# Perceiver encoder on one core: the feed-forward part and the last norm of the linear-attention encoder are worked inside its attention loop, and attention keeps to six accumulator banks

## The chip, the cores and the metric

The kernel runs on one core of a Trainium2 chip. The metric is the device time of one execution in microseconds (us). Engines are named as the profile names them: PE is TensorE (PEld its weight loads), DVE is VectorE, ACT is ScalarE, POOL is GpSimd, SP is SyncE, which issues the transfers. PSUM is the accumulator memory that PE writes, eight banks of 128 partitions x 512 floats.

## The reference

Input is x, 128 sequences of 32 rows with 128 features, and a context. Six blocks follow one another, each added to x. The change concerns the second alone, a Performer encoder layer:

```python
q, k, v = x @ Wq, x @ Wk, x @ Wv                  # 16 heads of 64
qf = exp(dash(q) - diag(q) - rowmax(dash(q))) + EPS_KERN
kf = exp(dash(k) - diag(k) - max over all of dash(k)) + EPS_KERN
attn = (qf (kf^T v)) / (qf sum(kf)),  attn_out = attn @ Wo
out1 = layernorm(x + attn_out, ln1_g, ln1_b)
h = elu(out1 @ W1 + b1)                           # 128 -> 512
return layernorm(out1 + (h @ W2 + b2), ln2_g, ln2_b)
```

Its x is the layer norm of the running x, and what it returns is added to the running x.

## The kernel before, in words

The 4096 rows are T = 32 tiles of 128 rows (four sequences each). `stage_performer` works the encoder in three blocks, one behind the other, with a barrier between them. In each block every engine has an order of its own, written out by hand, and the engines meet at semaphores.

The first block (`att`) makes the features of all keys once to find their largest value, and then runs `run(eng, step)`: step t works on tile t, and begins or ends its neighbours. The steps from -2 to 0 and from T-3 to T are written out; those between are a loop of two steps a turn, so that j = t % 2 picks between double buffers. In the numbering of the tile t, the PE order of a step is: output projection of tile t-1 (L1189), transposes of the query features (L1158 with `enc_eq`), transposes of the key features (L1158 with `enc_ek`), projection K of tile t+1 (`project`, L109 to L111: each product of two halved float32 operands is three passes), the scores (`scores`, L1168), projection V of t+1, projection Q of t+2, `values` (L1179), projection DQ of t+2 (the query features before the exponent). `project` names its pair of banks: BA = banks 0 and 1 for K and Q, BB = 2 and 3 for the query transposes and scores, BD = 4 and 5 for the key transposes and the output projection, BC = 6 and 7 for V and DQ. `values` writes banks 2 to 5.

DVE in a step: largest value of the query features of t+1 out of DQ's banks (`largest_q`, L1338), their sum with the diagonal (L1341), `residual` of t-1 (L1369), `exponent_q` of t+1 (L1345, reads DQ's banks and signals `sub_ok`), then `softened` of t (sum L1356, reciprocal L1358, division L1360, transpose L1363; it waits for the scores), `count` of t-1 (statistics, L1374), `diagonal` of the keys of t+1 (L1334), `exponent_k` (L1351), `diagonal` of the queries of t+2. ACT moves the projections out of PSUM, squares them and takes the exponents. POOL copies one tile a step (L1435).

The second block (`net`) takes groups of four tiles (NG = 8): it makes the folded weights and biases, the 32 tiles' mean and reciprocal deviation in one go (`rstd_dve`, L75 to L85, and a square root on ACT), normalises (`normal`, L1546), transposes (L1486), multiplies by W1 in two float32 passes of 512 columns for each quarter (`up`, L1492), builds the elu (ACT L1609 and L1616, DVE L1552), multiplies by W2 (`down`, L1499), adds (`result`, L1559) and counts (L1567). The third (`end`) does the last norm (L1672, L1681) and the sum into x (L1691, L1695). Behind it stands the barrier at L67 and then `stage_moe0`, whose POOL begins with a memset (L2133).

Of the kernel before, what the change touches and what calls it, by code (L numbers as in the profile page):

```python
# [1018 lines left out]
def stage_performer(nc, k, bufs, kept):  # L1019

    dn = float(DH0) ** -0.25
    with ExitStack() as ctx:
# [7 lines left out]
        with ExitStack() as att:  # L1030
# [19 lines left out]
            BA, BB, BD, BC = 0, 2, 4, 6  # L1050
# [48 lines left out]
            def run(eng, step):  # L1099

                def within(t):
                    return lambda d: 0 <= t + d < T

                for t in range(-2, 1):
                    step(t, t % 2, within(t), 1)
                with eng.Fori(0, (T - 4) // 2) as i:
                    step(2 * i + 1, 1, lambda d: True, i + 2)
                    step(2 * i + 2, 0, lambda d: True, i + 2)
                for t in range(T - 3, T + 1):
                    step(t, t % 2, within(t), T // 2)  # L1110

            @block.tensor
            def _(pe):
# [70 lines left out]
                def step(t, j, has, turns):  # L1184
# [7 lines left out]
                    if has(0):  # L1192
                        pe.wait_ge(eq_ok, t + 1)
                        turn(BB, eq[:, j, :], tq_mm)
                        pe.wait_ge(ek_ok, t + 1)
# [45 lines left out]
                pe.wait_ge(ev_ok, T)  # L1241
                run(pe, step)

            @block.scalar
            def _(act):
                half = dn * 0.5 ** 0.5

                def step(t, j, has, turns):
                    if has(0):
# [3 lines left out]
                        nc.scalar.activation(kfT[:, :], both(BD), ACT.Copy, bias=EPS_KERN).then_inc(kf_ok, 1)  # L1253
                    if has(1):
# [3 lines left out]
                        nc.scalar.activation(eq[:, 1 - j, :], eq[:, 1 - j, :], ACT.Exp).then_inc(eq_ok, 1)  # L1258
                    if has(0):
                        nc.scalar.activation(xr[:, j, :], at(k.x, t), ACT.Identity, bias=shift[:, bass.ds(t, 1)],  # L1260
                                             scale=k.rstd[:, bass.ds(t, 1)]).then_inc(xr_ok, 1)
                    if has(1):
                        act.wait_ge(v_mm, t + 2)
                        nc.scalar.copy(va[:, 1 - j, :], both(BC)).then_inc(va_ok, 1)
# [5 lines left out]
                    if has(0):  # L1270
                        act.wait_ge(o_mm, t + 1)
                        nc.scalar.copy(atT[:, :, :, :].rearrange("p c b n -> p b c n"),
                                       ps[:, BB:BB + SEQ, 0:256].rearrange("p b (c n) -> p b c n", n=N)).then_inc(at_ok, 1)
                    if has(1):
# [3 lines left out]
                        nc.scalar.activation(ek[:, :], ek[:, :], ACT.Exp, bias=negmx[:, 0:1]).then_inc(ek_ok, 1)  # L1278

# [51 lines left out]
            def _(dve):  # L1331
# [4 lines left out]
                def largest_q(t):  # L1336
                    dve.wait_ge(dq_mm, t + 1)
                    nc.vector.tensor_reduce(mx[:, :], heads(both(BC)), AX.X, ALU.max).then_inc(mx_ok, 1)  # L1338
# [4 lines left out]
                def exponent_q(t, j):  # L1343
                    dve.wait_ge(cc_ok, t + 1)
                    nc.vector.tensor_tensor(heads(eq[:, j, :]), heads(both(BC)),  # L1345
# [25 lines left out]
                def count(t):  # L1371
                    dve.wait_ge(res_ok, t + 1)
                    nc.vector.nop(nofuse=True)
                    nc.vector.bn_stats(at(k.stats, t), at(res, t))  # L1374

                def step(t, j, has, turns):
# [4 lines left out]
                    if has(1):  # L1381
                        exponent_q(t + 1, 1 - j)
                    if has(0):
                        softened(t)
                    if has(-1):
                        count(t - 1)
                    if has(1):
                        diagonal(dk, ksq, ksq_ok, dk_ok, t + 1)
                        exponent_k(t + 1, 1 - j, turns)
                    if has(2):  # L1390
                        diagonal(dq, qsq, qsq_ok, dq_ok, t + 2)

# [23 lines left out]
                for u in range(T):  # L1416
                    dve.wait_ge(ev_ok, u + 1)
                    nc.vector.tensor_reduce(tops[:, u:u + 1], held[u % NH][:, :], AX.X, ALU.max).then_inc(max_ok, 1)
                    if u % 4 == 2 and u // 4 < NG - 3:
                        normal(u // 4 + 3)  # L1420
                dve.wait_ge(max_ok, T)
# [8 lines left out]
            def _(pool):  # L1430
                def step(t, j, has, turns):
                    if has(2):
                        if has(0):
                            pool.wait_ge(v_mm, t + 1)
                        nc.gpsimd.tensor_copy(xt[:, j, :, :], xs[:, bass.ds(t + 2, 1), :, :].rearrange(  # L1435
                            "p t m q -> p (t m) q")).then_inc(xt_ok, 1)

# [12 lines left out]

                for g in range(NG):
# [4 lines left out]


        with ExitStack() as net:
            sb = lambda n, s: net.enter_context(nc.sbuf_tensor(f"net_{n}", s, F32))
            sem = lambda n: k.sem(f"net_{n}")  # L1460
            PART = 4
            NG = T // PART
            w1g, cols = sb("w1g", [P, FF]), bufs["cols"]
            up_bias, down_bias, b1p = sb("up_bias", [P, NF]), sb("down_bias", [P, NF]), sb("b1p", [P, NF])
            ones = sb("ones", [P, P])
            row = sb("row", [P, D])
            n4, nT = sb("n4", [P, 2, PART, D]), sb("nT", [P, 2, PART * P])
            low, m = sb("low", [P, 2, 512]), sb("m", [P, 2, 512])
            hT = sb("hT", [P, 2, NF, 512])
            (ln, w_mm, set_ok, n_ok, tr_mm, tr_ok, up_mm, low_ok, m_ok, h_ok, y_mm, y_ok, base_ok, sum_ok) = [sem(n) for n in (  # L1470
                "ln w_mm set_ok n_ok tr_mm tr_ok up_mm low_ok m_ok h_ok y_mm y_ok base_ok sum_ok").split()]
            T_B, U_B, Y_B = 0, 2, 6
            part_of = lambda a, g: a[:, bass.ds(PART * g, PART), :]
            block = net.enter_context(nc.Block())

# [1377 lines left out]
```

## Time and profile before

| what | value |
|---|---|
| median of three runs | 2589.21 us (2582.16 to 2591.71) |
| the profiled execution | 2586.26 us, its span 2584.2 us |
| PE busy | 2420.6 us, 94% of the span |
| DVE busy | 1671.5 us, 65% |
| ACT busy | 1451.9 us, 56% |
| POOL busy | 1048.9 us, 41% |
| the scores of tile 0 are first read by DVE at | 780.4 us |
| the scores of tile 31 are first read by DVE at | 1161.7 us |
| the third block of the encoder ends at | 1265.2 us |

The busy times are unions over the whole program, six blocks of which five are untouched. So the shares say little here, and the section of rows below keeps to the stretch from 760 to 1270 us. The columns in an answer of the timeline are start, length, engine, line, operation, what it writes and reads, how many instructions were merged, and in brackets the idle time before the first of them and who ended it.

### The profile page before, as it was taken

Reading aid. Unit: us, or ns where it says so; the run is one execution under the profiler, and the core shown is the slowest. Engines: PE = TensorE matmul, PEld = TensorE weight load, DVE = VectorE, ACT = ScalarE, POOL = GpSimd, SP = SyncE. Lnnn points to the kernel's source line nnn. Section 1 sums busy time; section 2 is a strip of 40 time slices with the busy share of each in tenths; the row PEclk is TensorE's granted clock in tenths of the full one; section 3 lists DMA queues with packets and bytes.
Section 4 is the critical chain, followed back from the end, with each engine's and each line's share of the span. In section 5 each row is a group of like instructions: output and inputs, shape, how many; then the busy total and the mean of one; then the engine's idle time right before and its main releaser. Section 6 shows DMA issues by size and latency. Waiting matters only on the chain. (4 is left out here: it accounts for less than half of the span.)

```text
span 2584.2 us, 95575 instructions
## 1 busy us (share of the span) xinstructions
PE 2420.6 (94%) x39473; PEld 2081.0 (81%) x39473; DVE 1671.5 (65%) x3176; ACT 1451.9 (56%) x4128; POOL 1048.9 (41%) x1152
## 2 busy tenths in 40 slices
PE   6999999999889999999589998999999989899999
PEld 5999999899768888886479996777777778888888
DVE  4777777677586767766555555777777757555553
ACT  4666666566466676665544445777777734422222
POOL 2444444344330000004344444666666623355555
PEclk9999999999999999998689998999999989799999
DMA  6544444444071111100200001101010010066564
GB/s 210 227 166 169 146 153 164 144 151 167 32 285 34 49 41 41 49 26 1 73 1 1 0 0 37 43 24 31 24 27 28 13 54 0 9 134 127 104 133 77
DMA packets 60323, 206.34 MB, mean 80 GB/s; under 512 B 6670, under 2 KB 20498, under 8 KB 51226
## 3 DMA queue, kind: packets, MB, share of 16 engines
q1 hardware_dynamic: 60188, 204.41, 25.9%
q8 instruction: 100, 1.64, 0.3%
q14 instruction: 35, 0.29, 0.0%
HBM read 182.88 MB, written 21.51 MB: 79 GB/s over the span
## 5 line engine op out<-in xcount | busy, mean ns | idle before, releaser
L579 POOL TENSOR_TENSOR l_pn<-l_probs,l_rden 128x1024 f32<-128x1024 f32 x128 | 242.3, 1893 | 409.0 <-DVE l_rden L415 409.0
L512 ACT ACTIVATE l_probs<-ps,l_nmax 128x257 f32<-128x257 f32 x512 | 236.3, 475 | 246.5 <-DVE l_nmax L409 231.5
L980 POOL TENSOR_TENSOR l_probs<-l_probs,l_rden 128x1024 f32<-128x1024 f32 x128 | 242.3, 1893 | 172.4 <-DVE l_rden L831 172.4
L916 ACT ACTIVATE l_probs<-ps,l_nmax 128x257 f32<-128x257 f32 x512 | 236.3, 474 | 59.7 <-DVE l_nmax L825 59.7
L409 DVE TENSOR_REDUCE l_nmax<-ps 128x2 f32<-128x514 f32 x256 | 165.2, 686 | 124.8 <-PE ps L291 124.8
L2735 POOL TENSOR_TENSOR m_hh<-m_hh,m_cb 128x512 f32<-128x512 f32 (+1 forms) x136 | 179.6, 1322 | 142.0 <-DVE m_hh L2687 128.7
L291 PE MATMUL ps<-l_ctxQ,l_q 32*128 32x257 f32 x3072 | 204.1, 394 | 12.8 <-ACT l_q L519 8.4
L2591 ACT ACTIVATE m_sg<-ps 128x512 f32<-128x512 f32 (+1 forms) x136 | 81.6, 600 | 220.0 <-PE ps L111 219.1
L825 DVE TENSOR_REDUCE l_nmax<-ps 128x2 f32<-128x514 f32 x256 | 165.5, 688 | 60.9 <-PE ps L717 57.2
L2687 DVE TENSOR_TENSOR m_hh<-ps,m_sg 128x512 f32<-128x512 f32 (+1 forms) x136 | 94.0, 691 | 167.4 <-PE ps L111 151.7
L836 DVE COPY l_pT<-ps 128x512 f32<-128x512 f32 x256 | 165.0, 686 | 52.2 <-PE ps L726 47.9
L291 PEld LDWEIGHTS ps<-l_ctxQ,l_q 32*128 32x128 f32 x3072 | 146.7, 185 | 38.2 <-issue 20.2
L1435 POOL CAST enc_xt<-enc_xs 128x256 fp32r (+1 forms) x32 | 12.8, 401 | 365.1 <-PE ps L111 365.1
L419 DVE STREAM_TRANSPOSE l_pT<-l_pn 128x1024 f32<-128x1024 f32 x128 | 157.5, 1230 | 0.0
L2529 PEld LDWEIGHTS ps<-m_wd,m_hh 128*128 128x128 f32 (+1 forms) x1088 | 141.3, 191 | 17.4 <-issue 6.4
L2529 PE MATMUL ps<-m_wd,m_hh 128*128 128x128 f32 (+1 forms) x1088 | 144.0, 275 | 2.6 <-POOL m_hh L2735 2.6
L726 PE MATMUL ps<-ident,l_probs 128*128 128x128 f32 x1024 | 133.2, 273 | 0.8 <-DVE x L845 0.4
L304 PE MATMUL ps<-l_pT,l_early 32*96 32x128 f32 x4096 | 124.1, 268 | 1.6 <-DVE x L429 1.0
L304 PEld LDWEIGHTS ps<-l_pT,l_early 32*96 32x96 f32 x4096 | 121.0, 158 | 5.2 <-issue 2.2
L304 PEld LDWEIGHTS ps<-l_pT,l_ctxK 32*96 32x96 f32 x4096 | 122.2, 160 | 3.2
L304 PE MATMUL ps<-l_pT,l_ctxK 32*96 32x128 f32 x4096 | 124.6, 269 | 0.0
L242 PE MATMUL ps<-l_xnT,l_A 128*128 128x128 f32 x768 | 120.1, 294 | 1.8 <-DVE l_xnT L399 0.4
(373 smaller groups left out, 6476.3 us busy)
## 6 DMA issues: line engine op xcount, KB each, us to landing
l_ctxQ<-in_ctx_q SPq DMA_DIRECT2D x32, 1542.0 KB, 6.5
l_ctxK<-in_ctx_k SPq DMA_DIRECT2D x16, 1536.0 KB, 6.5
l_early<-in_ctx_k SPq DMA_DIRECT2D x16, 1536.0 KB
enc_dash<-kept SPq DMA_DIRECT2D x32, 512.0 KB, 3.3
m_cb<-combined SPq DMA_DIRECT2D x32, 512.0 KB, 10.7
l_ctxT<-in_ctx_t SPq DMA_DIRECT2D x32, 385.5 KB, 3.4
m_cb<-combined SPq DMA_DIRECT2D x16, 768.0 KB, 15.6
kept<-enc_va SPq DMA_DIRECT2D x10, 512.0 KB, 3.1
```

What stands on the lines that cost most here:

```text
L291: last_i = nc.tensor.matmul(ps[:, S_B + hg, 0:NK], q1[r:r + N, j, c, b, :], ctxQ[r:r + N, j, c, b * NK:b * NK + NK], start=c == 0, stop=c ...
L304: last_i = nc.tensor.matmul(ps[0:C, W_B + h, 0:P], ctxK[j][r:r + N, b, m, :], pT[r:r + N, b % 2, :, m, :], start=m == 0, stop=m == NB - 1)
L409: nc.vector.tensor_reduce(nmax[:, par, 2 * half:2 * half + 2], ps[:, S_B + 2 * half:S_B + 2 * half + 2, 0:NK], AX.X, ALU.max, negate=True) ...
L419: nc.vector.transpose(pT[:, b % 2, :, :, :].rearrange("p g m n -> p (g m n)"), pn[:, b % 2, :, :].rearrange("p g n -> p (g n)")).then_inc( ...
L512: nc.scalar.activation(probs[:, par % 2, hg, :], ps[:, S_B + hg, 0:NK], ACT.Exp, bias=nmax[:, par, hg:hg + 1], accum_out=den[:, par, hg:hg ...
L579: nc.gpsimd.tensor_tensor(pn[:, b % 2, :, :], probs[:, b % 2, :, 0:NK - 1], rden[:, b, :, None].to_broadcast([P, HG, NK - 1]), ALU.mult).t ...
L825: nc.vector.tensor_reduce(nmax[:, b, 2 * half:2 * half + 2], ps[:, S_B + 2 * half:S_B + 2 * half + 2, 0:NK], AX.X, ALU.max, negate=True).t ...
L836: nc.vector.tensor_copy(pT[:, b % 2, kt, :], ps[:, T_B + kt, :]).then_inc(pt_ok, 1)
L916: nc.scalar.activation(probs[:, b, hg, :], ps[:, S_B + hg, 0:NK], ACT.Exp, bias=nmax[:, b, hg:hg + 1], accum_out=den[:, b, hg:hg + 1]).the ...
L980: nc.gpsimd.tensor_tensor(pr, pr, rden[:, b, :, None].to_broadcast([P, HG, K_W]), ALU.mult).then_inc(norm_ok, 1)
L2529: last = nc.tensor.matmul(ps[:, ACC + g % 2, n * P:n * P + D], hh[0:rows, v % 3, n * P:n * P + P], wd[0:rows, c, :], start=c + n == 0, sto ...
L2735: nc.gpsimd.tensor_tensor(h, h, cb[0:rows, c, :], ALU.mult).then_inc(h_ok, 1)
```

## The change

Three things are done.

1. **Banks.** BC is gone. V is projected into BD and DQ into BA. So K of tile t+1 now waits for `sub_ok`, DVE's last reading of DQ's banks (before, V waited for it); `values`, which writes banks 2 to 5, waits for `va_ok`, ACT's copy of V; DQ waits for `qsq_ok`, ACT's square of Q. Banks 6 and 7 are U_B and Y_B of the feed-forward part.
2. **The feed-forward part and the last norm go into the steps**, for pairs of tiles (PAIR = 2, 16 pairs). Pair g begins with `net_variances` in the even step 2g+2, is normalised, transposed and half multiplied by W1 in step 2g+3, gets the other half and W2 in step 2g+4, is added and counted (`net_result`) in 2g+5, gets its last norm (`net_final`, `net_added`) in 2g+6 and its last statistics (`net_count`) in 2g+7. The reciprocal square root is a power of -0.5 on POOL (`roots`), for two tiles at a time. The steps -2 to 6 and 29 to 37 are written out, the loop goes over i = 3 to 13. The second and the third block are gone; the folded weights are made before step -2. The buffers are those of the weights that are no longer used.
3. In `stage_moe0` POOL's memset stands behind the eight `high(g)` in place of ahead of them.

On PE the places are the head of an odd step, from the output projection of tile t-1 to the projection V of t+1. Before (steps 29 to 31, only the first instruction of each group is shown; L109 is the first pass of K, then of V):

```order
L1189 MATMUL ps<-enc_wo,enc_atT 128x128 [waits enc_at_ok]
...
L1158 MATMUL ps<-ident,enc_eq 128x128 [waits enc_eq_ok]
...
L1158 MATMUL ps<-ident,enc_ek 128x128 [waits enc_res_ok,enc_ek_ok]
...
L109 MATMUL ps<-enc_wide,enc_xt 128x512 [waits enc_qsq_ok]
...
L1168 MATMUL ps<-enc_kfT,enc_qfT 32x32 [waits enc_qf_ok,enc_kf_ok]
...
L109 MATMUL ps<-enc_wide,enc_xt 128x512 [waits enc_sub_ok]
```

The same place now (step 5; `enc_wkT` holds the normalised pair, `enc_wv` the folded W1):

```order
L1239 MATMUL ps<-enc_wo,enc_atT 128x128 [waits enc_at_ok]
...
L1182 MATMUL ps<-ident,enc_eq 128x128 [waits enc_eq_ok]
...
L1182 MATMUL ps<-ident,enc_ek 128x128 [waits enc_res_ok,enc_ek_ok]
...
L1213 MATMUL ps<-ident,enc_wkT 128x128 [waits enc_y_ok,enc_n_ok]
...
L109 MATMUL ps<-enc_wide,enc_xt 128x512 [waits enc_sub_ok]
...
L1192 MATMUL ps<-enc_kfT,enc_qfT 32x32 [waits enc_qf_ok,enc_kf_ok]
...
L1222 MATMUL ps<-enc_wkT,enc_wv 128x256 [waits enc_h_ok,enc_tr_ok]
```

The transposes of the pair (L1213) stand ahead of K and the scores, with a wait for DVE's `n_ok`, and K waits for `sub_ok`.

On DVE the place is the same odd step, from the residual of tile t-1 to the reading of the scores of t. Before, the residual (L1369), `exponent_q` (L1345) and `softened` (L1356) stand next to one another there. Now:

```order
L1479 TENSOR_TENSOR enc_res<-ps,enc_xr 128x128 [waits enc_wo_mm,enc_xr_ok]
L1455 TENSOR_TENSOR enc_eq<-ps,enc_cc 128x1024 [waits enc_cc_ok]
L1529 TENSOR_TENSOR enc_res<-ps,enc_res 128x256 [waits enc_base_ok,enc_y_mm]
L1535 BN_STATS stats<-enc_res 128x6 [waits enc_y_ok]
...
L1490 TENSOR_TENSOR enc_part_f<-stats 128x2 [waits enc_c2_ok]
...
L1494 TENSOR_SCALAR enc_f_mean<-enc_part_f 128x2 [waits enc_pf_ok]
...
L1499 SCALAR_TENSOR_TENSOR enc_f_var<-enc_part_f 128x2 [waits enc_pf_ok]
L1513 TENSOR_SCALAR enc_wkT<-enc_res,enc_a_rstd,enc_a_shift 128x128 [waits enc_base_ok,enc_tr_mm,enc_sa_ok]
...
L1466 TENSOR_REDUCE enc_den<-ps 128x16 [waits enc_s_mm]
```

Twelve instructions now stand between `exponent_q` and the scores' sum: one addition, two statistics, seven for the variance, and the two normalisations whose end is `n_ok`.

The diff, cut to its core:

```diff
-            BA, BB, BD, BC = 0, 2, 4, 6
+            BA, BB, BD = 0, 2, 4
+            U_B, Y_B = 6, 7
+            PAIR, NPAIR = 2, T // 2
...
-                for t in range(-2, 1):
-                    step(t, t % 2, within(t), 1)
-                with eng.Fori(0, (T - 4) // 2) as i:
...
+                for t in range(-2, 7):
+                    step(t, t % 2, within(t), (t + 1) // 2 + 1, (t - 1) // 2, paired((t - 1) // 2))
+                with eng.Fori(3, (T - 4) // 2) as i:
+                    step(2 * i + 1, 1, lambda d: True, i + 2, i, lambda d: True)
+                    step(2 * i + 2, 0, lambda d: True, i + 2, i, lambda d: True)
+                for t in range(T - 3, T + 6):
+                    step(t, t % 2, within(t), T // 2, (t - 1) // 2, paired((t - 1) // 2))
...
# PE, inside step
+                    if j == 0 and net(-1):
+                        net_up(i - 1, 1, True)
...
+                    if j == 1 and net(-1):
+                        net_turn(i - 1, net(-2))
                     if has(1):
-                        pe.wait_ge(qsq_ok, t + 2)
+                        pe.wait_ge(sub_ok, t + 2)
                         project(BA, W_K, 1 - j, k_mm)
...
                     if has(1):
-                        pe.wait_ge(sub_ok, t + 2)
-                        project(BC, W_V, 1 - j, v_mm)
+                        project(BD, W_V, 1 - j, v_mm)
+                    if j == 1 and net(-1):
+                        net_up(i - 1, 0, net(-2))
...
                         pe.wait_ge(pt_ok, t + 1)
+                        if has(1):
+                            pe.wait_ge(va_ok, t + 2)
                         pe.nop(nofuse=True)
                         values(j)
                     if has(2):
-                        if has(1):
-                            pe.wait_ge(va_ok, t + 2)
-                        project(BC, W_DQ, j, dq_mm)
+                        pe.wait_ge(qsq_ok, t + 3)
+                        project(BA, W_DQ, j, dq_mm)
+                    if j == 0 and net(-1):
+                        net_down(i - 1)
...
# DVE, inside step
                     if has(1):
                         exponent_q(t + 1, 1 - j)
+                    if j == 1 and net(-2):
+                        net_result(i - 2, net(-3))
+                    if j == 1 and net(-1):
+                        net_normal(i - 1, net(-2))
                     if has(0):
                         softened(t)
+                    if j == 0 and net(-1):
+                        net_elu(i - 1, 1)
                     if has(-1):
                         count(t - 1)
+                    if j == 0 and net(0):
+                        net_variances(i, net(-1))
...
+                    if j == 1 and net(-3):
+                        net_count(i - 3)
+                    if j == 1 and net(-1):
+                        net_elu(i - 1, 0)
```

The new functions on PE multiply pairs (a pair is PW = 256 columns):

```python
def net_up(g, half, again):
    pe.wait_ge(tr_ok, g + 1)
    if again:
        pe.wait_ge(h_ok, 2 * g + half)
    for c in range(2):
        at_c = (2 * half + c) * P
        last = nc.tensor.matmul(ps[:, U_B, c * PW:c * PW + PW], w1g[:, at_c:at_c + P], nT,
                                start=True, stop=True)
    last.then_inc(up_mm, 1)

def net_down(g):
    pe.wait_ge(h_ok, 2 * g + 2)
    for n in range(PAIR):
        for c in range(NF):
            last = nc.tensor.matmul(ps[:, Y_B, PW + n * P:PW + n * P + D], hT[:, c, n * P:n * P + P],
                                    w2[:, c, :], start=c == 0, stop=c == NF - 1)
    last.then_inc(y_mm, 1)
```

ACT has in an odd step `net_turned` ahead of the square of K, `net_below` behind the copy of V and `net_expo` behind the copy that ends `values`; in an even one `net_below` ahead of the square of K, `net_expo` behind the exponent of the queries, and `net_final` last. POOL has `roots` and `net_added` in an even step, `net_base` and `roots` in an odd one, behind its copy.

## Rows read from the trace of the kernel before

**Rows 1.** The page's slices of the span, TensorE's granted clock in tenths.

```profile
PEclk9999999999999999998689998999999989799999
```

**Rows 2.** Windows: length, busy us of PE, PEld, DVE, ACT, POOL, granted clock, DMA.

```profile
780.40:1161.70 381.30, 375.21 (x9654) 322.30 (x9654) 267.06 (x367) 258.49 (x278) 11.60 (x29) 0.99 0.13 40
1161.70:1265.20 103.50, 73.66 (x513) 54.71 (x512) 65.47 (x175) 60.53 (x110) 40.63 (x32) 0.82 0.00 1
```

**Rows 3.** Timeline of PE, one tile of the steady loop (start, us, engine, line).

```profile
998.30 1.95 PE L1189 MATMUL ps<-enc_wo,enc_atT 128*128 128x128 f32 x16
...
1000.09 1.04 PE L1158 MATMUL ps<-ident,enc_eq 128*128 128x128 f32 x8
...
1001.75 0.47 PE L109 MATMUL ps<-enc_wide,enc_xt 128*128 128x512 f32 x1
...
1003.32 1.29 PE L1168 MATMUL ps<-enc_kfT,enc_qfT 64*32 64x32 f32 x128
...
1004.54 0.51 PE L109 MATMUL ps<-enc_wide,enc_xt 128*128 128x512 f32 x1
...
1007.52 1.49 PE L1179 MATMUL ps<-enc_pT,enc_va 32*64 32x32 f32 x128
...
1010.44 1.95 PE L1189 MATMUL ps<-enc_wo,enc_atT 128*128 128x128 f32 x16
```

**Rows 4.** Timeline of DVE, the same tile.

```profile
1004.65 0.69 DVE L1356 TENSOR_REDUCE enc_den<-ps 128x16 f32<-128x512 f32 x1 [2.77 <-PE ps L1168]
...
1006.39 0.71 DVE L1363 STREAM_TRANSPOSE enc_pT<-enc_pr 128x512 f32<-128x512 f32 x1
...
1010.78 1.22 DVE L1338 TENSOR_REDUCE enc_mx<-ps 128x16 f32<-128x1024 f32 x1
...
1012.60 0.29 DVE L1369 TENSOR_TENSOR enc_res<-ps,enc_xr 128x128 f32 x1 [0.40 <-PE ps L1189]
...
1012.81 1.22 DVE L1345 TENSOR_TENSOR enc_eq<-ps,enc_cc 128x1024 f32<-128x1024 f32 x1
```

**Rows 5.** Timeline of the separate feed-forward stage, PE.

```profile
1223.75 1.88 PE L1492 MATMUL ps<-net_nT,net_w1g 128*128 128x512 f32 x4
```

**Rows 6.** Timeline of DVE in that stage.

```profile
1171.61 0.29 DVE L1369 TENSOR_TENSOR enc_res<-ps,enc_xr 128x128 f32<-128x128 f32 x1 [7.23 <-PE ps L1189]
...
1173.05 0.20 DVE L75 TENSOR_TENSOR half<-stats 128x32 f32<-128x32 f32 x1
...
1173.94 0.19 DVE L83 SCALAR_TENSOR_TENSOR var_eps<-half 128x32 f32<-128x32 f32 x1
...
1185.76 1.11 DVE L1546 TENSOR_SCALAR net_n<-enc_res,mean,rstd 128x128 f32<-128x128 f32 x4
...
1225.57 0.88 DVE L1567 BATCH_NORM_STATS2 stats<-enc_res 128x6 f32<-128x128 f32 x4
```

**Rows 7.** Groups of DVE in the next stage, a 256-column instruction out of PSUM.

```profile
L2011 DVE TENSOR_TENSOR m_sh<-ps,m_sa 128x256 f32<-128x256 f32 x24 | 10.2, 425 | 58.8 <-ACT m_sa L1932 58.8
```

**Rows 8.** Timeline of PE at two long gaps and one short one.

```profile
769.83 0.50 PE L109 MATMUL ps<-enc_wide,enc_xt 128*128 128x512 f32 x1 [2.14 <-DVE enc_eq L1345]
...
795.07 0.66 PE L1168 MATMUL ps<-enc_kfT,enc_qfT 64*32 64x32 f32 x37 [2.46 <-issue]
...
1620.64 0.48 PE L749 MATMUL ps<-l_last_w,l_last_bd 128*128 x2 [1.51 <-DMA l_last_w<-scratch]
```

**Rows 9.** Windows behind the two long gaps, and around the short one.

```profile
771.00:774.40 3.40, 3.40 (x10) 2.71 (x9) 1.23 (x1) 1.14 (x2) 0.43 (x1) 0.53 0.29 80
794.90:801.70 6.80, 6.63 (x98) 4.94 (x98) 4.87 (x7) 1.53 (x2) 0.40 (x1) 0.52 0.01 2
1590.00:1622.00 32.00, 27.34 (x269) 20.14 (x268) 21.27 (x41) 22.12 (x83) 18.99 (x21) 1.00 0.39 97
```

**Rows 10.** Timeline at the head of the next stage, POOL and DVE.

```profile
1266.62 2.66 POOL L2133 MEMSET l_ctxT<- 1x3084 f32 x1 [3.10 <-POOLq L67]
...
1267.33 1.99 DVE L79 TENSOR_SCALAR mean<-half 128x32 f32<-128x32 f32 x1
```

More of the change, by code:

```diff
@@ L1241, in _ @@
                 pe.wait_ge(ev_ok, T)
+                for c in range(NF):
+                    last = nc.tensor.matmul(ps[:, U_B, c:c + 1], w1[:, c * P:c * P + P], cols[:, 1:2], start=True, stop=True)
+                last.then_inc(w_mm, 1)
+                pe.wait_ge(set_ok, 1)
+                for c in range(NF):
+                    last = nc.tensor.matmul(ps[:, Y_B, 0:D], net_ones[:, :], w2[:, c, :], start=c == 0, stop=c == NF - 1)
+                last.then_inc(w_mm, 1)
+                pe.wait_ge(sum_ok, 4)
+                pe.wait_ge(set_ok, 2)
                 run(pe, step)
@@ L1246, in _, with net_turned, net_below, net_expo @@
                 half = dn * 0.5 ** 0.5
-                def step(t, j, has, turns):
+                def net_turned(g):
+                    act.wait_ge(tr_mm, g + 1)
+                    nc.scalar.copy(nT, ps[:, Y_B, 0:PW]).then_inc(tr_ok, 1)
+                def net_below(g, half, again):
+                    act.wait_ge(up_mm, 2 * g + half + 1)
+                    if again:
+                        act.wait_ge(m_ok, 2 * g + half)
+                    for c in range(2):
+                        cc = 2 * half + c
+                        last = nc.scalar.activation(low[:, c, :], ps[:, U_B, c * PW:c * PW + PW], ACT.Relu,
+                                                    bias=down_bias[:, cc:cc + 1], scale=-1.0)
+                    last.then_inc(low_ok, 1)
+                def net_expo(g, half, again):
+                    act.wait_ge(low_ok, 2 * g + half + 1)
+                    if again:
+                        act.wait_ge(h_ok, 2 * g + half)
+                    nc.scalar.activation(m, low, ACT.Exp, scale=-1.0).then_inc(m_ok, 1)
+                def net_final(g, again):
+                    act.wait_ge(sf_ok, g + 1)
+                    if again:
+                        act.wait_ge(x_ok, g)
+                    for n in range(PAIR):
+                        t = PAIR * g + n
+                        last = nc.scalar.activation(f4[:, n, :], at(res, t), ACT.Identity, bias=norm_f[3][:, bass.ds(t, 1)],
+                                                    scale=norm_f[2][:, bass.ds(t, 1)])
+                    last.then_inc(fa_ok, 1)
+                def step(t, j, has, turns, i, net):
                     if has(0):
@@ new lines, in net_variances, with net_normal @@
+                def net_variances(g, again):
+                    dve.wait_ge(ct_ok, PAIR * g + PAIR)
+                    variances(g, norm_a, part_a, pa_ok, va_set, again)
+                def net_normal(g, again):
+                    dve.wait_ge(sa_ok, g + 1)
+                    if again:
+                        dve.wait_ge(tr_mm, g)
+                        dve.wait_ge(base_ok, 2 * g)
+                    for n in range(PAIR):
+                        t = PAIR * g + n
+                        last = nc.vector.tensor_scalar(n4[:, n, :], at(res, t), norm_a[2][:, bass.ds(t, 1)],
+                                                       norm_a[3][:, bass.ds(t, 1)], ALU.mult, ALU.add)
+                    last.then_inc(n_ok, 1)
@@ L1377, in step, with net_count @@
+                def net_count(g):
+                    dve.wait_ge(x_ok, g + 1)
+                    nc.vector.nop(nofuse=True)
+                    for n in range(PAIR):
+                        t = PAIR * g + n
+                        nc.vector.bn_stats(at(k.stats, t), at(k.x, t))
+                def step(t, j, has, turns, i, net):
                     if has(1):
@@ L1430, in _, with step @@
             def _(pool):
-                def step(t, j, has, turns):
+                def step(t, j, has, turns, i, net):
                     if has(2):
@@ L2139, in _ @@
                 high(g)
+            pool.wait_ge(xh_ok, NG)
+            nc.gpsimd.memset(next_ones, 1.0).then_inc(row_ok, 1)
+            pool.wait_ge(row_ok, 1)
             for n, src in enumerate((w1, w3)):
```

361 lines of the change are left out of this document (140 added, 221 removed).

## The prediction

> **What bounds the kernel now.** I read the page's slices first: TensorE's granted clock is at or near its full level (2.4 GHz) through the whole middle of the span, with dips in three slices around the encoder's start and its end [rows 1]. Then the windows, because the change touches one stretch only: from the first scores read (780.4 us) to the last (1161.7) PE is busy 375.2 of 381.3 us at a granted clock of 0.99, while DVE is busy 267 and ACT 258. Behind it the rest of tile 31, the feed-forward part and the last norm take 103.5 us, in which PE is busy 73.7 at 0.82 [rows 2]. So the attention steps are bound by PE, and the 103.5 us is what the change can spread among them. Then the timelines of one tile. From one output projection to the next it takes 1010.44 - 998.30 = 12.14 us, and PE has no gap [rows 3]. DVE is closer to its limit than its share says: it starts on the scores at 1004.65 and has work without a break until the exponent's subtraction ends at 1012.81 + 1.22 = 1014.03, but for 0.40 us ahead of the residual; only then does it wait, 2.8 us, for the next scores [rows 4]. The reader is to see a chain of 9.4 us in which every link is DVE's.
>
> **The sum.** It is made against the profiled execution, 2586.3 us; the median of the runs, 2589.2, lies 2.9 above.
>
> *Removed and put at the end.* The 103.5 us of [rows 2] go. In their place stands what is left behind the last scores. Tile 31's own rest (softmax, values, output projection) took 1171.6 + 0.3 - 1161.7 = 10.2 us, at the low clock for the larger part [rows 6]. Then pairs 14 and 15 are finished without cover: half of 14's elu and its second product, its result and variance on DVE, pair 15's normalisation, transposes, two halves of W1 with their three passes on ACT and DVE each, W2, result, variance, root, last norm, sum, statistics. In that chain PE has about 6 us at full clock (16 passes of W2 twice at 1.8 each, eight of W1 and more), DVE about 9, and ACT and POOL some 9 in pieces of about half a microsecond. Together 31 if all runs at full clock and 38 to 40 if PE runs at half rate, which it did behind 1161.7. I take 38: **-65.5**.
>
> *PE's added work.* A float32 pass of 512 columns of W1 takes (1.88 - 0.59) / 3 = 0.43 us where 0.59 is the last one's own length [rows 5], so a pass of 256 columns 0.215; a pair has eight, 1.7 us. Its 16 passes of W2 cost what the 16 of the output projection cost, 1000.09 - 998.30 = 1.8, and two transposes 0.2 (eight take 0.87: sixteen lie between 1000.09 and 1001.75) [rows 3]. That is **3.8 us a pair** with edges. Two tiles without it take 24.3, with it 28.1.
>
> *PE's added waits.* I lay DVE's order against PE's, time 0 being DVE's start on the scores. **Even to odd step.** DVE: softmax and transpose to 2.4 (1006.39 + 0.71 - 1004.65, less the overlap), one elu half of two instructions 0.8 (0.43 for 256 columns out of PSUM [rows 7], twice), statistics 0.25, `net_variances`, then the key and query diagonals and the exponent, 3.6, to 8.15. The variance is the seven instructions of L75 to L83, 1173.05 to 1174.13, 1.08 us on 32 columns [rows 6]; these small ones hardly depend on the width, and I take 1.05. Largest value and sum go to 9.6. The residual waits for the output projection, and PE now has W2's 16 passes ahead of that: on PE values end at 4.8, DQ at 6.3, W2 at 8.1, the projection at 9.9, and 0.4 later DVE can go on (the same 0.4 lies between the projection's end on PE, 1012.2, and the residual at 1012.60 [rows 3, 4]). Residual and subtraction end at 11.7. `net_result` is 0.43 + two statistics of 0.22 with 0.15 of semaphores [rows 6] + another 1.05, and two normalisations at 0.28 each (1.11 / 4) end at 14.4. PE is through with both transposes at 11.5 and stands ahead of `net_turn` until then: **2.9 us**. Behind it come 0.2 + K 1.57 + scores 1.22 + 0.1 until DVE may start again: 17.5. **Odd to even.** No result, no W2. K comes at 11.0 on PE, the subtraction ends at 10.7: 0.3 of slack, so PE sets the pace, 12.1 + 1.8 for the two halves of W1 that fall there, 13.9. `values` also waits 0.3 us in the even step, since ACT has the square, two exponents and the residual's scaling ahead of V's copy. A pair takes 31.4 in place of 24.3. There are 14 such full pairs between the scores of tile 3 and of tile 31, 14 x 7.15 = 100; the first three steps have a wait of K for `sub_ok`, 0.2 each (the ring 9.4 + 1.6 + 1.3 = 12.35 against 12.14), and the first variance and normalisation, 2.5 in all: **+102.5**.
>
> *The clock.* In this trace an idle PE was followed by half rate: a gap of 2.14 us by 3.4 us at a granted clock of 0.53, one of 2.46 us by 6.8 us at 0.52, whereas one of 1.51 us left it at 1.00 [rows 8, 9]. Those figures say that the lower level is 1.2 GHz and that a gap of 2.9 us is of the kind behind which it comes. PE's next work, transposes, K and scores, is on the ring, so each us at half rate costs half a us. Bounds: 0 if it never falls, 14 x 3.4 = 48 if each gap brings 6.8 us. I take half, since the gap is one piece in 31 us and may be met at any point: **+24**. The Trainium skill, TensorE: Matmul & The Clock Gate, section Why this matters for your kernels, advises against idle gaps of over about 3 us between bursts, so by it 2.9 us would just pass and this term would be 0, the sum 2628. The trace does not agree: its two shorter gaps did not pass.
>
> *The start.* The folded weights stand ahead of step -2: 16 passes on PE and six small instructions on DVE, 2.5 us, of which the old place is already removed. DQ of tiles 0 and 1 waits for the square of Q (1 us each) and K of 0 for the subtraction. **+5**, bounds 3 and 8. *The next stage.* The memset of 2.66 us stretched a small DVE instruction to 1.99 us [rows 10]; later it may meet others: **-1**, bounds -2 and 1. *POOL, ACT, SP.* All that POOL did for this part is within the 40.6 us it was busy in the second window, 2.5 a pair of 31, and all that ACT did within 60.5, under 4 a pair [rows 2]; POOL's roots are needed 9 us after they can start. SP's transfers of the kept features are two steps ahead and unchanged. At nothing, and it stays so unless a power on POOL takes more than those 9 us.
>
> Sum: -65.5 + 102.5 + 24 + 5 - 1 = +65; 2586.3 + 65 = 2651, and I say **2652 us**, 2.5% over the profiled execution.
>
> **The rivals.**
>
> (A) The same ring, and the clock holds. For it: the gap is one in 31 us, and PE is dense around it. Against: the two gaps of [rows 8]. 2652 - 24 = 2628.
>
> (B) The same ring, and every pair pays 6.8 us at half rate. For it: 2.46 us had just that. 2652 + 24 = 2676.
>
> (C) Faster: DVE's chain does not reach PE. The place is `net_turn` in the odd step. If small instructions overlap and DVE works ahead, `n_ok` comes before PE is through with the key transposes; the point is 2.9 us less DVE work in that step than I count, which is more than the whole `net_result` (2.1). Then only PE's work is added, 14 x 3.8 + 1 = 54, the clock stays at 1.00, the tail is 31 and the start 2: -103.5 + 31 + 54 + 2 - 1 = -17.5, 2569. For it: PE was the bound before. Against: [rows 4], where DVE has 2.8 us to spare in a tile that is to take 5.6 us a pair more.
>
> (D) As C with my tail and start, or with a third of the waits: 2577 to 2598, no change. Work is then only moved, since PE's 54 us in the steps nearly eat the 65.5 of the end.
>
> (E) The change does not do what it says because POOL holds it up: a power of two columns costs many us. The nearest row has none. At 12 us a power, POOL would be the bound from the point where roots and sums exceed 31 us a pair, over 2700.
>
> **How the numbers follow.** A measurement of this kernel tells about 0.5% (13 us) from no change. Chances: forecast 0.50, A 0.22, B 0.15, C 0.05, D 0.05, E 0.03. The forecast, A and B are all slower, and E too: 0.90 slower, 0.05 the same, 0.05 faster. The range goes from A with the variances' small instructions a quarter shorter (14 x 0.5 = 7), a tail of 34 and a start of 3 (2628 - 7 - 4 - 2 = 2615), with half a us a pair below that for waits counted too long (2608), to B with a start of 8 and 0.8 us more a pair (2676 + 3 + 11 = 2690). It leaves C, D, E and what is left of the ends out.
>
> **What would show it.** Right: PE waits 2 to 4 us in every odd step at the transposes L1213, released by DVE L1513; a pair takes 30 to 35 us from scores to scores, odd steps and even steps 4 us apart; the window of the steps is over 480 us and the rest under 45; the granted clock in the steps is under 0.97 (forecast), or 1.00 (A), or near 0.89 (B). Wrong: no idle time at L1213 and a pair in 28 us (C); POOL L1647 of several us (E); PE waiting instead at `values` for ACT's copy of V.

## The result and the profile after

The changed kernel takes 2661.96 us (median of four runs, 2657.94 to 2669.55) beside 2586.39 for the kernel before on the same chip: a ratio of 1.031 with an interval of 1.0285 to 1.0335. Slower, as forecast. Four more runs in a later set gave 1.0302 (below). Two executions that show a lower granted clock (0.83 and 0.74, 2760.7 us of the kernel before and 3038.5 us of e7) are left out of the ratios. The profiled execution has a span of 2655.5 us against 2584.2, so +71.3.

From the page of the changed kernel, PE's busy time and the slices of its granted clock ([rows 1] has those of before):

```profile
PE 2442.0 (92%) x39537; PEld 2102.5 (79%) x39537; DVE 1694.0 (64%) x3415; ACT 1452.9 (55%) x4164; POOL 1093.8 (41%) x1265
...
PEclk9999999999999999999859999999999989899999
```

The windows of the changed kernel from the first scores read to the last, and from there to the encoder's end; they answer to [rows 2], with the same columns:

```profile
787.20:1305.10 517.90, 459.68 (x10021) 390.62 (x10021) 342.99 (x722) 309.64 (x403) 85.60 (x156) 0.93 0.09 30
1305.10:1345.00 39.90, 18.62 (x194) 15.14 (x194) 12.92 (x53) 9.72 (x21) 10.72 (x19) 0.69 0.00 1
```

The reader is to see two things: the stretch behind the last scores shrank from 103.5 us to under 40, and the steps, which were all PE (375.2 of 381.3), now have 58 us in which PE is idle, at a granted clock of 0.93 in place of 0.99. Term by term, with the encoder's last instruction at 1343.3:

| term | predicted | the two traces |
|---|---|---|
| the program ahead of the encoder's last feature reduction (761.8 to 759.8) | 0 | -2.0 |
| start (from that reduction to the first scores read, 18.6 to 27.4) | +5 | +8.8 |
| steps, first to last scores (381.4 to 517.9) | +102.5 + 24 = +126.5 | +136.5 |
| behind the last scores (103.5 to 38.2) | -65.5 | -65.3 |
| encoder's end to the next stage's first product (6.3 to 4.9) | -1 | -1.4 |
| the rest of the program (1312.7 to 1307.3) | 0 | -5.4 |

**The ring.** PE's timeline of the changed kernel around the transposes of a pair, in an odd step of the loop:

```profile
1061.54 1.04 PE L1182 MATMUL ps<-ident,enc_eq 128*128 128x128 f32 x8
1062.50 1.06 PE L1182 MATMUL ps<-ident,enc_ek 128*128 128x128 f32 x8
1066.77 0.43 PE L1213 MATMUL ps<-ident,enc_wkT 128*128 128x128 f32 x2 [3.20 <-DVE enc_wkT L1513]
1066.95 0.48 PE L109 MATMUL ps<-enc_wide,enc_xt 128*128 128x512 f32 x1
...
1069.34 1.55 PE L1192 MATMUL ps<-enc_kfT,enc_qfT 64*32 64x32 f32 x128
```

DVE's timeline of the same step:

```profile
1062.28 1.21 DVE L1455 TENSOR_TENSOR enc_eq<-ps,enc_cc 128x1024 f32<-128x1024 f32 x1
1063.41 0.41 DVE L1529 TENSOR_TENSOR enc_res<-ps,enc_res 128x256 f32 x1
1064.01 0.54 DVE L1535 BATCH_NORM_STATS2 stats<-enc_res  x2 [0.20 <-DVE enc_res L1529]
1064.73 0.16 DVE L1490 TENSOR_TENSOR enc_part_f<-stats 128x2 f32 x1 [0.18 <-DVE stats L1535]
...
1065.67 0.16 DVE L1499 SCALAR_TENSOR_TENSOR enc_f_var<-enc_part_f 128x2 f32 x1
1066.03 0.60 DVE L1513 TENSOR_SCALAR enc_wkT<-enc_res,enc_a_rstd,enc_a_shift 128x128 f32 x2 [0.20 <-issue]
1070.93 0.69 DVE L1466 TENSOR_REDUCE enc_den<-ps 128x16 f32<-128x512 f32 x1 [4.30 <-PE ps L1192]
```

DVE finishes the subtraction at 1063.5, just when PE is through with the key transposes. Then come `net_result`, its variance and the normalisation, 1063.41 to 1066.63, and PE starts 0.14 later. Behind them the roles turn: DVE waits 4.30 us for the scores. The two engines take turns, each idle while the other works on the ring. PE's waits in the steps of the changed kernel, summed (us, times, longest):

```profile
PE ps L1213 <- DVE enc_wkT L1513: 41.1, 15, 3.2
PE ps L1203 <- issue: 8.2, 4, 2.5
PE ps L1192 <- issue: 5.9, 3, 2.1
PE ps L1203 <- ACT enc_va L1368: 1.1, 1, 1.1
```

41.1 us belong to the wait that the forecast named. The second and third line were not in the sum (see e6).

**The clock.** Windows of the changed kernel that begin where a gap of PE ends: three of the loop's gaps of 3.20 us (they end at 1033.92, 1066.77 and 1099.44), and one of 2.33 us that ends at 1265.32:

```profile
1033.92:1040.70 6.78, 6.78 (x147) 5.45 (x148) 2.30 (x5) 3.55 (x5) 3.39 (x6) 0.79 0.00 0
1066.77:1073.50 6.73, 6.73 (x148) 5.33 (x149) 2.46 (x6) 3.68 (x6) 3.40 (x6) 0.75 0.00 0
1099.44:1106.80 7.36, 7.36 (x147) 5.84 (x147) 2.50 (x6) 3.32 (x5) 3.40 (x6) 0.62 0.00 0
1265.32:1272.12 6.80, 6.80 (x147) 5.35 (x148) 2.18 (x4) 3.42 (x5) 3.00 (x5) 0.75 0.01 2
```

Twice what is missing from 1.00 is the share of the time at half rate (1.2 GHz): 2.8, 3.4 and 5.6 us behind the three gaps of 3.20 us, and it falls on K and the scores first. Behind the nine gaps of 3.20 or 3.21 us that follow one another from 967 to 1233 us it is 2.8 to 6.1 us, 4.4 in the mean.

The length of a gap alone doesn't decide it. The loop's gap just before those nine was as long, and the clock held behind it; behind a gap of 1.82 us that ends at 885.07 (PE L1203 <- issue) it fell, two us later:

```profile
935.86 0.43 PE L1213 MATMUL ps<-ident,enc_wkT 128*128 128x128 f32 x2 [3.17 <-DVE enc_wkT L1513]
```

```profile
935.86:942.66 6.80, 6.80 (x152) 5.35 (x152) 3.59 (x6) 4.48 (x7) 3.40 (x6) 1.00 0.00 0
885.07:891.87 6.80, 6.80 (x45) 6.44 (x46) 2.71 (x3) 2.83 (x4) 1.79 (x3) 0.75 0.26 80
```

The second run of the same kernel (a2) has two such gaps of 3.17 and 3.19 us with the clock at 1.00 behind them, and nine of 3.20 or 3.21 with half rate. What decides between them is open. The Trainium skill, TensorE: Matmul & The Clock Gate, section Why this matters for your kernels, names gaps of over about 3 us as those to avoid; ten of the eleven such gaps in the steps agree, the one at 935.86 does not, and shorter ones did not all pass.

### The profile page after: what moved, and what is told of

Same layout as the page of the kernel before. It is cut to its first block and busy times, and to the rows that moved or that the text cites. A ratio compares the mean times of both kernels' runs of the same rounds, so it can differ in the third digit from the quotient of the medians.

```text
span 2655.5 us, 96619 instructions
## 1 busy us (share of the span) xinstructions
PE 2442.0 (92%) x39537; PEld 2102.5 (79%) x39537; DVE 1694.0 (64%) x3415; ACT 1452.9 (55%) x4164; POOL 1093.8 (41%) x1265
## 5 line engine op out<-in xcount | busy, mean ns | idle before, releaser
L109 PE MATMUL ps<-enc_wide,enc_xt 128*128 128x512 f32 x256 | 122.6, 479 | 7.7 <-DVE enc_eq L1455 5.1
```

Source lines behind the costliest of these rows:

```text
L109: nc.tensor.matmul(out, left[0], right[0], start=True, stop=False)
```

## The experiments

Every ratio is to the kernel before on the same chip. e1, e2, e4 and e5 shared a chip (before: 2579.8 us), the others another (2582.9).

### e1_turn_late: the transposes of the pair behind the scores

```diff
 # PE, odd step
-                    if j == 1 and net(-1):
-                        net_turn(i - 1, net(-2))
...
                         scores()
+                    if j == 1 and net(-1):
+                        net_turn(i - 1, net(-2))
```

On ACT `net_turned` moves likewise, behind the exponent of the queries.

> The changed kernel with one thing moved: the transposes of the pair (and ACT's copy of them) stand behind the scores in place of ahead of K. DVE then works net_result and the normalisation (2.7 us behind the subtraction) while PE works K and the scores (2.9 us), where before DVE waited. Theory of the ring: the interval from an even to an odd scores reading falls from 18.7 to 14.7 us, the next one is 14.1, a pair 28.8 in place of 33.1, the clock stays at 1.00 in the loop, and the time falls by 14 x 4.3 = 60 us to about 2600. Rival, the waits are only moved (PE then waits for ACT or for the subtraction as long as it did for n_ok): 2650 to 2662.

Measured: 2606.1 us, ratio 1.0106 (1.005 to 1.0162). A pair takes 28.75 us (28.8 was forecast), in place of 33.1. 250 us of the loop, its first turn at their head, and one pair of it, in the windows of this kernel:

```profile
900.00:1150.00 250.00, 242.99 (x5544) 208.13 (x5533) 195.78 (x417) 175.07 (x230) 49.27 (x90) 1.00 0.11 36
1013.87:1042.62 28.75, 28.41 (x650) 24.34 (x650) 23.05 (x50) 20.48 (x28) 6.05 (x11) 1.00 0.11 36
```

DVE does the same work at the same place; only PE no longer stands and waits for it, since K and the scores go first:

```profile
1041.21 1.29 PE L1192 MATMUL ps<-enc_kfT,enc_qfT 64*32 64x32 f32 x128
1042.84 0.43 PE L1213 MATMUL ps<-ident,enc_wkT 128*128 128x128 f32 x2 [0.34 <-DVE enc_wkT L1513]
```

So the place of `net_turn` costs two thirds of the loss: 1.031 becomes 1.011, and in the traces the steps go from 517.9 to 456.7 us, a difference of 61 (14 pairs x 4.35). The wait and the low clock go together here; e4 parts them.

### e4_gap_filled: the gap stays, the clock doesn't fall

```diff
 def net_turn(g, again):
+    if again:
+        pe.wait_ge(h_ok, 2 * g)
+        for _ in range(13):
+            matmul(ps[:, U_B, 0:P], ident, ident, start=True, stop=True)
     pe.wait_ge(n_ok, g + 1)
```

> The changed kernel with 13 multiplications of the identity with itself (26 passes, 2.9 us) on PE ahead of its wait for n_ok, into bank 6, which is free there. They fill the gap and give nothing. Theory (each gap is followed by 3.4 or 6.8 us at half rate, which costs half of that on the ring): the granted clock in the loop goes from 0.94 to 1.00, a pair from 33.1 to 31.5 us, the time falls by about 22 us to 2640. Rival, the half rate falls where PE had slack: no change, 2662. Rival, the filling itself is late and in the way: slower than 2665.

Measured: 2641.6 us, ratio 1.0228 (1.0167 to 1.0289), a pair in 31.49 us, both as forecast. PE's timeline with the filler in the gap, and a window of one pair:

```profile
1027.05 1.06 PE L1182 MATMUL ps<-ident,enc_ek 128*128 128x128 f32 x8
1027.95 3.07 PE L1212 MATMUL ps<-ident 128*128 128x128 f32 x26
1031.24 0.44 PE L1217 MATMUL ps<-ident,enc_wkT 128*128 128x128 f32 x2 [0.22 <-DVE enc_wkT L1517]
```

```profile
1016.74:1048.23 31.49, 31.27 (x677) 27.29 (x678) 22.87 (x49) 20.48 (x29) 6.07 (x11) 1.00 0.10 33
```

The transposes start no earlier, but the clock is 1.00 and a pair is 33.1 - 31.5 = 1.6 us shorter. That is the clock's share; the wait's is 31.49 - 28.75 = 2.7. Half of the 4.4 us at half rate would be 2.2; one reason for the lower cost is that small products lose less: K's passes of 512 columns start 0.43 us apart at half rate against 0.23, but the 128 products of the scores take 1.55 us (changed kernel) against 1.29 (e1). Rival A (the clock holds by itself, 0 a pair) is out, and so is B (3.4 us a pair).

### e5_variance_behind: 1.4 us less between the subtraction and `n_ok`

```diff
 # DVE, odd step
                         net_result(i - 2, net(-3))      # now without its variance
                         net_normal(i - 1, net(-2))
                         softened(t)
+                    if j == 1 and net(-2):
+                        net_result_variance(i - 2, net(-3))
```

> The changed kernel with the seven small instructions of the variance in net_result moved behind softened, so that n_ok comes 1.3 us earlier. Ring theory: DVE has the same work between two readings of scores of an even tile, so at full clock a pair loses only the 0.3 us of slack (31.4 to 31.1); the wait at the pair's transposes falls from 3.2 to 1.9 us and about 1 us of wait turns up ahead of K in the even step. If the clock then holds, 31.1 a pair and 2634; if not, 32.8 and 2658. Rival, the gap at the transposes is itself the cost: 1.3 us and the half rate less a pair, 30.0, below 2622.

Measured: 2625.9 us, ratio 1.0178 (1.012 to 1.0236), a pair in 30.47 us, between the two. A window of one pair, and one of the work behind the gap that ends at 1020.03:

```profile
1023.13:1053.62 30.49, 28.70 (x651) 24.30 (x652) 22.73 (x50) 20.52 (x28) 6.08 (x11) 1.00 0.10 34
1020.00:1026.80 6.80, 6.76 (x152) 5.35 (x152) 3.25 (x13) 4.48 (x7) 2.19 (x4) 1.00 0.00 0
```

PE's gap is 1.78 us (3.20 before) and the clock holds, behind this one and the loop's other eight of 1.78 or 1.79 us. Even to odd falls by 1.36 us against e4, odd to even rises by 0.34: the variance was not moved out of DVE's work, only behind the scores, and the odd step takes all but a third of a us of it. So its slack was about 1.0 us, not the 0.3 of my sum. The wait ahead of K in the even step that was expected does not show: between 950 and 1230 us PE waits at L1213 alone.

### e2_banks_only: the kernel before with V in BD and DQ in BA

```diff
-            BA, BB, BD, BC = 0, 2, 4, 6
+            BA, BB, BD = 0, 2, 4
-                        pe.wait_ge(qsq_ok, t + 2)
+                        pe.wait_ge(sub_ok, t + 2)
                         project(BA, W_K, 1 - j, k_mm)
...
-                        project(BC, W_V, 1 - j, v_mm)
+                        project(BD, W_V, 1 - j, v_mm)
...
-                        project(BC, W_DQ, j, dq_mm)
+                        project(BA, W_DQ, j, dq_mm)
```

DQ's wait for `qsq_ok` and the wait of `values` for `va_ok` come with it, as in the change.

> The kernel before with attention on six banks and nothing else: V into BD, DQ into BA, and the three waits that go with it. Ring theory: 12.35 us from scores to scores in place of 12.13, so +6.6 over 31 tiles, and +3 at the start, in sum some 2596, +0.4%, at full clock. Rival, ACT's copy of V holds values up in every tile by 0.3 us or more on top: +15 or more. Rival, the waits are all covered: no change.

Measured: 2598.0 us, ratio 1.0063 (1.0036 to 1.009), 12.36 us a tile (12.35 forecast, 12.14 before). It was to add 9.6 us and added 18.2 (9 to 23 by the interval); it meets the 2596 only because the kernel before is 6.5 us faster in this set than the 2586.3 that the forecast was built on. PE's timeline of the key transposes and K, then DVE's row of the subtraction that K waits for:

```profile
1003.17 1.04 PE L1158 MATMUL ps<-ident,enc_ek 128*128 128x128 f32 x8
1004.15 0.51 PE L109 MATMUL ps<-enc_wide,enc_xt 128*128 128x512 f32 x1
```

```profile
1002.88 1.21 DVE L1345 TENSOR_TENSOR enc_eq<-ps,enc_cc 128x1024 f32<-128x1024 f32 x1
```

K starts 0.98 us behind the start of the key transposes, and 0.06 behind the subtraction's end. In the kernel before it was 1001.75 [rows 3] less the start of this row, 0.79:

```profile
1000.96 1.04 PE L1158 MATMUL ps<-ident,enc_ek 128*128 128x128 f32 x8
```

That is 0.2 us a tile, with PE shown busy throughout. The start has the gap that the changed kernel has:

```profile
779.08 0.77 PE L109 MATMUL ps<-enc_wide,enc_xt 128*128 128x512 f32 x1 [4.07 <-DVE enc_eq L1345]
```

In [rows 8] it was 2.14. From DVE's last feature reduction to the first scores read it takes 26.2 us here (it begins at 768.44, they are read at 794.67), 18.6 in the kernel before and 17.1 in e3, which has the same steps. So 7.6 to 9.1 us are added at the start, not 3. Against 12.36, a pair of e1 is 28.75 - 24.72 = 4.0 us longer, 0.34 of it waited: PE's added work is 3.7, where the sum has 3.8.

### e3_memset_only: the kernel before with the memset moved

```diff
-            nc.gpsimd.memset(next_ones, 1.0).then_inc(row_ok, 1)
-            pool.wait_ge(row_ok, 1)
...
                 high(g)
+            pool.wait_ge(xh_ok, NG)
+            nc.gpsimd.memset(next_ones, 1.0).then_inc(row_ok, 1)
+            pool.wait_ge(row_ok, 1)
```

> The kernel before with the third part of the change alone, POOL's memset behind the eight casts of the next stage. My step: -1 us, between -2 and +1, so no difference that can be measured. Rival: the 5.4 us that the span behind the encoder lost are the memset's, then -5 and -0.2%.

Measured: 2579.8 us, ratio 0.9991 (0.9964 to 1.0017): no difference that ten runs can tell. Its interval, -9 to +4 us, holds both -1 and -5, so the time doesn't settle it. In the traces, PE's idle time ahead of the next stage's first product falls from 28.22 to 26.66 us, close to the forecast 1. The 5.4 us need no memset: in the program behind that product, where the code is otherwise the same, the profiled executions of all kernels of this study took from 1306.5 us (e1) to 1319.9 (e7), and this one 1314.2 against 1312.7 before. What makes them differ is open.

### e6_four_more: e1 with four more steps written out

```diff
-                for t in range(-2, 7):
+                for t in range(-2, 11):
-                with eng.Fori(3, (T - 4) // 2) as i:
+                with eng.Fori(5, (T - 4) // 2) as i:
```

This tests the gaps that end by "issue", in which PE waits for nothing that the profile shows.

> The kernel with the transposes behind the scores (2606 us), its loop begun two turns later, so that four more steps are written out and nothing else is changed. PE has gaps of 1 to 2.4 us that end by issue in the first turn of the loop and none in steps 4 to 6 ahead of it. If they belong to the entry into the loop, they move back by four steps and the time stays within 3 us. If they belong to the amount of code that is met for the first time, two more pairs have them: +6 us or more.

Measured: 2617.2 us, ratio 1.0143 (1.0109 to 1.0178). The intervals of e1 and e6 overlap, and the two ran on different chips, so I go by the traces, one of each: first to last scores take 469.7 us against 456.7, +13.0, of which 11.8 lie between the scores of tiles 8 and 12, beside the steps 7 to 10 that were written out. The same 62 us, loop in e1 and written out in e6. e1:

```profile
920.00:982.00 62.00, 61.33 (x1343) 53.08 (x1341) 48.94 (x103) 42.44 (x57) 13.86 (x25) 1.00 0.12 41
```

e6, window and PE's timeline there:

```profile
920.00:982.00 62.00, 55.40 (x1157) 47.61 (x1156) 38.49 (x82) 36.44 (x50) 11.17 (x20) 0.93 0.09 28
```

```profile
944.83 0.34 PE L1192 MATMUL ps<-enc_kfT,enc_qfT 64*32 64x32 f32 x26 [2.10 <-issue]
...
952.38 0.89 PE L1203 MATMUL ps<-enc_pT,enc_va 32*64 32x32 f32 x39 [1.64 <-issue]
```

PE stops in the middle of 128 small products of one kind, for which nothing has to be awaited. The queue that carries instructions moved, in e6 between 920 and 982 (packets, MB, share):

```profile
q8 instruction: 8, 0.13, 0.9%
```

In e1 it moved nothing in that window. In the changed kernel, steps 0 to 8, of which 7 and 8 are the loop's first turn (787.2 to 938.97), against ten pairs behind them (938.97 to 1269.84):

```profile
q8 instruction: 22, 0.36, 1.0%
...
q8 instruction: 1, 0.02, 0.0%
```

So the gaps come with code that runs for the first time, and with instructions being fetched. That the fetch is what PE waits for is the reading I take; it is not shown, for no run moved the fetch alone.

### e7_head_tail: e1 with the start and the end repaired

```diff
+            dq_pair = lambda u: 6 if isinstance(u, int) and u <= 2 else BA   # DQ of tiles 0 to 2
+                        if dq_pair(t + 1) == BA: pe.wait_ge(sub_ok, t + 2)
+                        else: pe.wait_ge(qsq_ok, t + 2)                      # K, as before the change
 # folded weights: made beside the last features' largest values, not behind them
 # behind step 31, ahead of net_turn and net_down:
+                            for _ in range(8):
+                                matmul(ps[:, BA, 0:P], ident, ident, start=True, stop=True)
```

> The kernel with the transposes behind the scores (2606 us), its start and its end shortened: the folded weights are made beside the last features, DQ of tiles 0 to 2 goes to banks 6 and 7, which are free until step 3 (K then waits for the square as it did before), and eight multiplications of the identity fill PE's waits behind step 31. My terms: -5 us at the start, -4 at the end, some 2597, still over the kernel before by 0.6%, for PE has 60 us more in the steps and the first steps and the loop's entry have their gaps.

Measured: 2598.0 us, ratio 1.0066 (1.0044 to 1.0088). The total is as forecast, its terms are not. Its windows, first to last scores and from there to the next stage's first product:

```profile
774.99:1236.70 461.71, 438.95 (x10019) 376.01 (x10020) 344.73 (x722) 308.80 (x401) 85.93 (x155) 0.98 0.11 34
1236.70:1276.73 40.03, 21.34 (x244) 18.34 (x245) 16.13 (x66) 12.86 (x27) 11.29 (x21) 0.77 0.04 12
```

Against the kernel before, the first scores are read 5.4 us earlier, the end is 69.8 us shorter, and the steps are 80.4 longer. Against e1, the start (last feature reduction to first scores) falls from 28.9 to 15.5 us, a little of it because the folded weights now stand ahead of that reduction; the end falls by 3.0; and the steps take 5.0 more. The start was put at -5 and gave 13: the banks of the first DQs had cost more there than was thought. It is the best version of the change that ran, and still slower than the kernel before by 0.4 to 0.9%.

### a2_again: the changed kernel once more

> The changed kernel itself, as the base of the others on this chip: 1.031 of the kernel before, within 0.5%.

Measured: 2661.2 us, ratio 1.0302 (1.0263 to 1.034), as expected.

## Why the prediction was right, step by step

**What bounds.** "A chain of 9.4 us in which every link is DVE's" decided the case. DVE's share of the span is 64%, and yet 3.2 us of its work on this chain cost PE 3.2 us; e1 shows that the same work costs next to nothing when PE has K and the scores to do meanwhile.

**The tail.** 38 taken, 38.2 measured. It was the slow end of the bounds that came true: PE has four gaps of 2.5 to 2.6 us there and runs mostly at half rate (0.69 in the window).

**PE's added work.** 3.8 us a pair forecast, 3.7 found (e1 against e2).

**The wait at `net_turn`.** 2.9 forecast, 3.20 measured. The mis-sized piece is DVE's block of twelve instructions: 2.7 us in the sum, 3.2 in the trace. The same block outside the loop, in step 29 of the changed kernel:

```profile
1262.83 0.41 DVE L1529 TENSOR_TENSOR enc_res<-ps,enc_res 128x256 f32<-128x256 f32 x1
...
1263.86 0.16 DVE L1490 TENSOR_TENSOR enc_part_f<-stats 128x2 f32<-128x2 f32 x1
...
1264.66 0.60 DVE L1513 TENSOR_SCALAR enc_wkT<-enc_res,enc_a_rstd,enc_a_shift 128x128 f32<-128x128 f32 x2
```

There it takes 1265.26 - 1262.83 = 2.4 us and PE's gap is 2.33. In the loop the instructions are about as long, but pauses of 0.18 to 0.20 us stand at three of the waits between them (ahead of L1535, L1490 and L1513), where 0.15 in all had been taken. The forecast 0.3 us at `values` did not come: the only wait for ACT's copy of V was 1.1 us, once. Both errors cancel, which is luck: a pair was to take 31.4 + 1.7 = 33.1 us, and the ten pairs from 938.97 to 1269.84 took 330.87 / 10 = 33.09 (nine of the gaps in the loop, the tenth in step 29).

**The odd step's slack.** 0.3 in the sum, about 1.0 by e5. It changed nothing in the forecast, since nothing was put there.

**The clock.** 1.7 us a pair forecast, as half of what [rows 8, 9] allowed, and 1.6 measured by e4. The number is right and its reason only in part. Half was taken because a gap might be met at any point; in these ten pairs each gap was followed by half rate, for 4.4 us in the mean of nine, between the 3.4 and 6.8 of the sum. And a us at half rate cost less than the half us that was put, since the scores' small products lose only a fifth. These two offset each other. Rival A was not as weak as two falls on record made it: the gap at 935.86 held the clock, and so did one of 2.12 us in e3, at the very place of the 2.14 us of [rows 8]. The third window of [rows 9] ends 1.4 us behind its gap, too early to tell; the trace keeps the clock at 1.00 up to 1632, so the reading stands.

**What the sum left out.** The steps cost 10 us more than forecast, and none of it is in the ten pairs from 938.97 on: 8.8 lie between the scores of tiles 3 and 9 (108.1 us for three pairs), 2.2 in the pair behind tile 29. PE's gaps that end by "issue" add up to 16.0 us in the steps (the two rows of the waits above, and three smaller ones), where before they were 2.8 (and 4.7 in e3's trace of the same steps): 11 to 13 us more, with half rate behind some, and part of it hidden where PE would have waited for DVE anyway. The section on the clock used the one such gap of [rows 8] as a sign of how the clock behaves, and the sum never as a cost that written-out code brings. The change writes out 18 steps (-2 to 6, 29 to 37) where before had 7. By e6 four more cost 13 us; a term for them was missing.

**The start.** +5 forecast with bounds of 3 and 8; this term was mis-sized. The first scores come only 6.8 us later, but the program ahead of them was 2.0 us faster in this execution. DVE's last feature reduction, first in the kernel before, then in the changed one:

```profile
761.77 1.22 DVE L1418 TENSOR_REDUCE enc_tops<-enc_ksq 128x1 f32<-128x1024 f32 x1
```

```profile
759.81 1.22 DVE L1601 TENSOR_REDUCE enc_tops<-enc_ksq 128x1 f32<-128x1024 f32 x1
```

From there to the first scores it is 780.4 - 761.8 = 18.6 us and 787.2 - 759.8 = 27.4, so +8.8; a2 has 28.9. K of tile 0 waited 4.07 us for the subtraction, in place of 2.14. The banks alone bring most of it (e2, 26.2), and with the first three DQs in banks of their own it is gone (e7, 15.5). **POOL** is not the bound (rival E): a power took 0.69 us on two columns. **C and D** fell with the wait at L1213; e1 is C's "only PE's work is added" made true, and it came out at +1.1%, not at -0.7%, because of the start (C has 2 us for it), the 0.2 us a tile from the banks and the written-out code.

## What to carry to other kernels

A low busy share is no licence to put work on an engine: look at where the work would stand between its input from the bound engine and its output to it, and have the bound engine do everything else it can before it waits for the newcomer (the same instructions, with two calls moved, were 14 x 4.35 us). If the bound engine is already full, pouring a stage into its loop can win only that stage's idle time; here 14 x 3.8 = 53 us of work went in for 65 saved, and the start, 0.2 us a tile and the price of new code ate more than the 12. Count written-out steps as a cost, and a gap on the bound engine as its length plus what may run at the lower clock behind it. Measure a stretch from a mark inside the same trace: the time ahead of it differs between executions (the last feature reduction began at 753.6 us in e3 and at 768.4 in e2).

## What the runs showed of the hardware

- PE stopped for up to 2.5 us at a time, for nothing that the profile shows, in the middle of runs of small products in code met for the first time; all such stops are 16 us in the 152 + 35 us of these steps of the changed kernel, and 2.8 us in all steps of the kernel before. Four more written-out steps cost 13 us (e6).
- Small DVE instructions on 128x2 values take 0.15 us and start 0.08 us apart, but in the loop a wait between two of them cost up to 0.2 us: 3.2 us for a block that took 2.4 outside.
- A power of two columns on GpSimd took 0.69 us, a multiplication there 0.20.
- The clock fell behind nine gaps of 3.20 or 3.21 us in a row and behind one of 2.33, but held behind one of 3.17 in the same trace, and behind nine of 1.78 or 1.79 in e5; behind one of 1.82 it fell. The half rate lasted 2.8 to 6.1 us. At half rate the 128 small products of the scores took 1.55 us in place of 1.29.
